# Statistics of the feed-forward input earlier in the vector queue, and one feed-forward matmul group ahead of a projection

## The reference, cut to what matters

```python
# x: (8 batches, 512 tokens, 128), float32
x = layernorm(x + attention(x))                   # 16 heads, causal
for i in range(6):                                # DEPTH
    x = attn_layer(shift_tokens(x), ...) + x      # local attention, 16 heads of 64
    x = ffn_layer(shift_tokens(x), ...) + x
x = layernorm(x0 + x)

def shift_tokens(t):                              # second half of the features moves one token down
    a, s = split(t, 2, -1)
    return concatenate([a, pad(s, one token in front)[:, :-1]], -1)

def attn_layer(x, Wqkv, qs, ks, Wo):
    q, k, v = split(x @ Wqkv, 3, -1)              # 1024 columns each
    q, k = rotary(l2norm(q) * qs), rotary(l2norm(k) * ks)
    return local_attention(q, k, v) @ Wo          # windows of 32, look one back

def ffn_layer(x, g, b, W1, b1, W2, b2):
    xn = (x - mean) / sqrt(var + 1e-5) * g + b
    a, gate = split(xn @ W1 + b1, 2, -1)          # 341 columns each
    return a * gelu(gate) @ W2 + b2
```

## Time and profile before

| | |
|---|---|
| median of 3 runs | 3530.5 us |
| the profiled execution | 3530.5 us |
| its span, first to last instruction | 3528.7 us |
| PE, PEld, DVE, ACT, POOL busy | 97%, 82%, 85%, 87%, 71% |
| mean granted TensorE clock | 0.997 |

### The profile page before, as it was taken

One profiled execution on the slowest core, in us unless ns is written; L12 is line 12 of the kernel. 1 busy time (PEld: TensorE's weight loads), 2 busy tenths in 40 slices (PEclk: granted clock), 3 DMA queues, 4 the chain that ended last, 5 costly groups with the idle time before them and its releaser, 6 DMA issues. The chain is left out here.

```text
span 3528.7 us, 177745 instructions
## 1 busy us (share of the span) xinstructions
PE 3421.5 (97%) x70388; PEld 2879.3 (82%) x70388; DVE 3012.0 (85%) x7016; ACT 3058.8 (87%) x10549; POOL 2500.7 (71%) x2057
## 2 busy tenths in 40 slices
PE   8999989999999999999999999999999999999998
PEld 5666678888888888888888888888888888888877
DVE  8999988888888888887888888888888888888886
ACT  8999978888888888888888888888888888888886
POOL 0111188887878778787787877878878788787774
PEclk9999999999999999999999999999999999999999
DMA  2000011111111111121111121112111111111111
GB/s 103 8 6 18 5 55 52 49 40 43 55 55 51 42 43 46 52 57 47 43 45 49 50 56 46 43 42 55 57 47 45 42 47 53 45 43 50 49 42 44
DMA packets 177474, 160.59 MB, mean 46 GB/s; under 512 B 113933, under 2 KB 124813, under 8 KB 176397
## 3 DMA queue, kind: packets, MB, share of 16 engines
q1 hardware_dynamic: 176653, 149.22, 15.0%
HBM read 25.71 MB, written 4.19 MB: 8 GB/s over the span
## 5 line engine op out<-in xcount | busy, mean ns | idle before, releaser
L1544 POOL TENSOR_TENSOR a_rn<-a_ssqc,a_minus_half 128x16 f32<-128x16 f32 x384 | 1114.8, 2903 | 310.8 <-DVE a_ssqc L1751 309.8
L1428 ACT ACTIVATE late<-bank,a_negmax 128x64 f32<-128x64 f32 x3072 | 964.0, 341 | 68.2 <-DVE a_negmax L1705 66.5
L1562 POOL TENSOR_TENSOR a_r<-a_u,a_rn 128x512 f32<-128x512 f32 x768 | 802.4, 1045 | 51.7 <-issue 1.3
L1428 ACT ACTIVATION_READ_ACCUMULATOR late<-bank,a_negmax 128x1 f32 x3072 | 719.3, 234 | 0.0
L1717 DVE TENSOR_TENSOR a_u<-bank,a_rot_c 128x512 f32<-128x512 f32 x768 | 524.4, 683 | 190.4 <-ACT a_sq L1404 189.8
L1551 POOL TENSOR_TENSOR a_PN<-late,a_erec 128x256 f32<-128x256 f32 x768 | 489.5, 638 | 245.7 <-DVE a_erec L1758 226.4
L1726 DVE TENSOR_TENSOR a_v<-bank,a_rot_s 128x512 f32<-128x512 f32 x768 | 522.3, 680 | 0.0
L1733 DVE TENSOR_TENSOR a_u<-a_u,a_v 128x1024 f32<-128x1024 f32 x384 | 470.1, 1224 | 35.5 <-DVE a_v L1726 0.5
L1404 ACT ACTIVATE a_sq<-bank 128x512 f32<-128x512 f32 x768 | 466.8, 655 | 16.4 <-PE bank L1013 15.9
L1411 ACT ACTIVATE a_QK<-bank 128x512 f32<-128x512 f32 x768 | 465.2, 606 | 4.2 <-PE bank L1054 1.9
L1054 PE MATMUL bank<-ident,a_r 128*128 128x128 f32 x3072 | 463.7, 274 | 5.3 <-ACT late L1396 1.8
(11 more groups left out here) (190 smaller groups left out, 7768.7 us busy)
## 6 DMA issues: line engine op xcount, KB each, us to landing
a_V_sh<-a_V_nat SPq DMA_DIRECT2D x384, 192.0 KB, 2.4
a_V_sh<-a_V_nat SPq DMA_DIRECT2D x192, 64.0 KB, 2.3
late<-in_qkv SPq DMA_DIRECT2D x20, 384.0 KB, 3.9
a_x_sh<-X SPq DMA_DIRECT2D x48, 128.0 KB
a_V_sh<-a_V_nat SPq DMA_DIRECT2D x192, 32.0 KB, 2.1
a_x_sh<-X SPq DMA_DIRECT2D x48, 127.0 KB
late<-X SPq DMA_DIRECT2D x47, 128.0 KB
late<-X SPq DMA_DIRECT2D x47, 127.0 KB
```

Source lines behind the costliest of these rows:

```text
L1428: ins = act.activation(E[:, s.par, k, :], scores[:, hp, col:col + KW], ACT.Exp, bias=negmax[:, s.par, k:k + 1], accum_out=esum[:, s.par, k ...
L1544: pool.tensor_tensor(rn[:, a.par, :], ssqc[:, a.par, :], minus_half[:, :], ALU.pow).then_inc(S["rn"], 1)
L1562: pool.tensor_tensor(heads(r[:, a.par, half]), heads(u[:, a.par, half]), rn[:, a.par, mm * 2 * HG:(mm + 1) * 2 * HG].unsqueeze(2).to_broad ...
```

## The change

Four things move, nothing is added or removed:

- TensorE, p = 6: the up group `up(n, p, 0, 1, p_ta)` goes ahead of the second projection instead of behind it.
- VectorE, p = 0: `stats(n)` goes from behind the reciprocals to the place between `sines(b, 1)` and `add(b)`.
- VectorE, p = 1: `norm(n)` goes from behind `add(b)` to the place ahead of it.
- GpSimd: `deviation` goes from p = 1, ahead of `power`, to p = 0, behind the first `units`.

```diff
@@ TensorE, cycle @@
                 if p == P_X:
                     up(n, p, 2, 1, p_ta)
+                if p == P_VALUES:
+                    up(n, p, 0, 1, p_ta)
                 if p == P_TURN:
                     turn(n)
                 project(n, p, 1)
-                if p == P_VALUES:
-                    up(n, p, 0, 1, p_ta)
@@ GpSimd, cycle @@
                 probs(pair_at(n, p, LAG_S + 1), 1)
-                if p == P_NORM and n >= 2:
-                    deviation(n - 2)
                 power(pair_at(n, p, LAG_R))
                 units(pair_at(n, p, LAG_R), 0)
+                if p == 0 and n >= 2:
+                    deviation(n - 2)
@@ VectorE, cycle @@
                 clamp(b)
                 sines(b, 1)
+                if p == P_NORM:
+                    norm(n)
                 if p == P_X:
                     residual(n)
+                if p == 0:
+                    stats(n)
                 add(b)
...
                 if p == P_TURN:
                     turned(n)
-                if p == P_NORM:
-                    norm(n)
                 cosines(a, 0)
                 sines(a, 0)
...
                 reciprocals(s, 0)
                 reciprocals(s, 1)
-                if p == 0:
-                    stats(n)
```

## The result

The changed kernel is slower: the median of four runs is 3626.2 us (3620.3 to 3633.5), against 3530.8 us of the kernel before on the same chip. The ratio is 1.027, with a 95% interval of 1.0249 to 1.0292. The forecast was 3615 us with a range of 3598 to 3645. The profiled execution took 3632.6 us, 102 us more than that of before.

A forecast was written before the change was run, and what follows sets the result against it. TensorE, busy for 97% of the span, was taken as the bound. On 3530.5 us, part 1 added 84, Parts 2 to 4 added 0, and 1 was added for later loads: 3615 us, range 3598 to 3645.

The forecast's parts named there:

- The load: The load of f_sh lands 10.19 us after R, the residual's end; the moved stats idles 2.9 us for it.
- The step that carried the sign: At p = 0 VectorE reaches stats at 7.29 us after the residual's end, before the load is there: slower, chance 0.94.
- rival B: The load is there in time, so VectorE's idle is filled: faster by 32 us, 3498 us; chance 4%.
- part 1: Moving stats at p = 0: its wait for the load delays TensorE by 1.81 us an iteration, +84 us in all.
- (b): The second projection of p = 1 waits for VectorE's sines and starts 1.81 us later; this decides the term.
- (a): TensorE's transposes of r at the end of p = 0 wait on stats, add and units: a stall of 1.9 us.
- Parts 2 to 4: norm ahead of add, deviation behind the first units, up group ahead of the second projection at p = 6: 0 each.
- part 1's stall: TensorE stands 1.9 us at p = 0, hiding the up group's 0.3 us; without it, 14 us would count.
- shorter than 1.80, hence I take no fall: The new wait ahead of the transposes, 1.4 to 1.6 us by the profile's measure, brings no clock fall.
- Rival A: The clock falls as well, 1.7 us each: 3693 us if in each iteration, 3641 in a third; chance 13%.

The follow-up runs named there:

- e4: The changed kernel with the DMA of 127 partitions cut into 112 and 15, for both shifted loads: 3496.9 us, ratio 0.9904.
- e5: The kernel before with only the load cut into 112 and 15 partitions: 3530.8 us, ratio 0.9997.
- e7: The changed kernel with stats one place further back, behind add and ahead of cosines: 3549.8 us, ratio 1.0053.
- e8: The changed kernel with only the up group back behind the second projection: 3633.7 us, ratio 1.0288.
- e9: The kernel before with stats and norm moved, deviation and the up group at their old places: 3632.8 us, ratio 1.0289.
- e2: The changed kernel with only stats put back behind the reciprocals: 3538.9 us, ratio 1.0022.
- e1: The kernel before with only the up group moved ahead of the second projection at p = 6: 3537.1 us, ratio 1.0019.
- e3: The kernel before with only stats moved ahead of add: 3651.9 us, ratio 1.0341.
- e6: The changed kernel with the load cut into 112 and 15 partitions and the up group at its old place: 3488.3 us, ratio 0.9880.
- e12: The kernel before with stats moved ahead of add, and norm between cosines(a, 0) and sines(a, 0): 3652.3 us, ratio 1.0340.
- e13: The kernel before with stats moved ahead of add, and three short memsets ahead of add at p = 1: 3652.0 us, ratio 1.0340.

## Why the prediction was right, and where it was not

**The load.** Forecast was `stats` at R + 10.19 with 2.8 to 2.9 us of idle, 132 us in all; measured are R + 10.13, 2.64 and 121 us in 46 waits. e4 and e5 show that this and nothing else turns a gain of 34 us into a loss of 95. The step that carried the sign held. The prediction set a fit of the Trainium skill beside rival B, from "DMA: Bandwidth & Descriptors", section "Anatomy of one DMA — SWDGE (gpsimd) path". That section is about DMAs issued from GpSimd, and SyncE issues this load, so the measured time doesn't speak against the page.

**The chain to TensorE, part 1.** That (b) decides was right, shown by e7. Its size was not: R + 17.56 was forecast and R + 17.23 measured. From the start of `stats` to the projection it takes 7.10 us instead of 7.37, since `stats` hands over after 1.40 us instead of 1.65. L549 took 0.45 us in the old place and takes 0.17 in the new; I had taken the block's length over as it was. So the term is 1.45 us an iteration and not 1.81, 67 us and not 83. (a) was 1.29 us of idle, 1.4 to 1.6 forecast, for the same reason. The first iteration paid 2.2, forecast 2.5.

**Parts 2 to 4.** All were put at 0, and are, to within 2 us in the runs. e8 and e9 together show `deviation` at 0, e8 shows the up group at 0 beside part 1's stall (the ordinary iteration is the same), and e2 against e1 shows `norm` at 0 without the move of `stats`. Behind it, `norm`'s place is worth 19 us (e3 to e9), which I hadn't seen. Without part 1's stall I had put the up group at 0.3 us an iteration, 14 us; e1 gives 6.5 and e6 8.6. The mechanism was there, the size half: some of TensorE's delay has cover until the next iteration.

**The clock.** The step that failed is this one: the stall is "shorter than 1.80, hence I take no fall". It is shorter, and the clock falls behind it in 15 of the 36 steady iterations (without the first, the last four and those in which a layer begins), once in each. The prediction used one wait with a fall behind it as a bound below which none comes. The trace of before has four waits of 1.80 us, and a fall behind two of them. Here is one of the others, and the stretch behind it (columns as in rows 6), with the clock at 1.00:

```profile
3236.25 0.47 PE L1011 MATMUL bank<-a_wh,a_xh 128*128 128x512 f32 x1 [1.80 <-DVE a_v L1726]
```

```profile
3236.30:3239.70 3.40, 3.40 (x59) 2.64 (x61) 2.57 (x5) 2.91 (x9) 3.27 (x3) 1.00 0.00 0
```

So the length of a wait alone didn't decide, and no bound could be read from it. Rival A gave 1.7 us per fall; in the iterations it is 0.9, since the slower clock swallows the wait that follows. The range took in falls in a third of the iterations, and that share was about right; the price of one was about half.

**The layers' first iterations.** Not priced at all: at five of them four more instructions of VectorE, 1.67 us, stand in chain (b), and two falls come with the longer wait. The second projection is late by 2.9 us there instead of 1.48, and the other 2.1 us come behind it, where the clock is low: 3.6 us each beyond the common part, 18 us in all. I had read an ordinary iteration and taken 46 of them.

**The sum.** 85 us were forecast; 102 came in the profiled execution, 95 in the median. The term of part 1 was 17 us too high, and 35 us of falls, layer changes and the end were missing. The two errors partly cancelled, so 3615 lies nearer to 3626 than its working deserves.

## What to carry to other kernels

Before an instruction that waits for a transfer is moved forward, find in the trace when the data land, not when the issue ends: an iteration in which the wait was once open shows it. If they land later than the new place, ask first whether the transfer can be cut otherwise; here that turned the same change from +95 us into -34. And price a repeated change in every kind of iteration that there is, with the clock's answer to each new stall.

## What the runs showed of the hardware

- The load of `f_sh` as 128, 127 and 1 partitions was complete 10.1 us after the residual (10.1 to 10.4 in the 46 loads), and the DMA of 127 held SyncE's next issue for 6.5 us, at a DMA share of 0.08. The third DMA could be issued only behind it, its issue ended at R + 8.0, so the 10.1 us hold both: the slow DMA and the one that it kept waiting. The trace's landing events of the load's semaphore fit this: seventeen at about R + 2, one at R + 8.4 to 8.6, four from R + 9.0 on; which DMA each belongs to isn't marked. With the 127 cut into 112 and 15 partitions the last event came at R + 4.1 to 5.0 (e4), and the four issues took 0.65 to 0.94 us each in the median. The Trainium skill ("DMA: Bandwidth & Descriptors", section "Why a DMA increments its semaphore by 16 and not by 1") takes for the number of engines the largest divisor of the partitions up to 16: one for 127, 16 for 112, 15 for 15. The runs agree: a load has 22 landing events before the cut, and 42 to 52 after it.
- A wait of 1.3 to 1.5 us of TensorE ahead of the transposes was followed by 3.4 us at the 1.2 GHz level in 15 of 36 steady iterations of the changed kernel and in 13 of 36 of e8 (1.4 to 1.6 us), 1.6 to 2.0 us behind its end; in the others, with a like wait, by none. Behind the waits of 1.80 us of the kernel before a fall came in two of four, with those of 2.2 us at the layer changes of the changed kernel in five of five; in the steady iterations of e7 (1.05 us, 1.2 at most) never. What decides between like cases wasn't tried.
- GpSimd's `power` took 3.93 us instead of 2.90 wherever VectorE's `add` had started 0.05 or 0.06 us ahead of it (46 times in each of e3, e12 and e13), and 2.90 in every other place of all the runs. The reverse is there too: the rotary table instruction of VectorE that started 0.04 us behind GpSimd's `units` took 1.15 us instead of 0.28 (45 times, five in each of nine runs). By the Trainium skill ("SBUF — State Buffer", section "SBUF: two separate sides") a VectorE instruction with two inputs in SBUF and a GpSimd instruction lock a pair of ports against each other, and the one that comes second waits for the whole of the first. Both of these fit. A third case doesn't: in the changed kernel `add` started at 1611.86, in the midst of `power`, and took its usual 1.23 us, as it did wherever it started 0.2 us or more behind `power`. These are correlations; e13, which was to show the cause, did not reach it.
- The same small VectorE instruction (L549, 128x4) took 0.45 us ahead of the reduction of the maxima (L1705) and 0.17 us ahead of `add`. That the reduction reads PSUM isn't the difference: in e7 it took 0.17 us ahead of `cosines`, which reads PSUM too. What is, wasn't tried.
